# First attention: scores of two heads in the two halves of 64 rows of the matmul array

## The chip, the cores and the metric

The kernel runs on one core of one Trainium2 chip. The metric is the device time of one execution in microseconds (us). TensorE (PE) multiplies, VectorE (DVE), ScalarE (ACT) and GpSimd (POOL) work on what it leaves in PSUM and on SBUF, and SyncE (SP) and ScalarE issue DMA transfers.

## The reference, cut to what matters

Eight sequences of 512 tokens with 128 features pass through four layers, each an attention-like part and a feed-forward part. The first layer is

```
xn = layernorm(x)
q, k, v = xn @ wq.T + wq_b, xn @ wk.T + wk_b, xn @ wv.T + wv_b      # 16 heads of 8
q, k = rope(q), rope(k)
scores = einsum('bhqd,bhkd->bhqk', q, k) / sqrt(8)                 # no mask: 512 x 512 a head
attn = softmax(scores); out = einsum('bhqk,bhkd->bhqd', attn, v)
x = x + out * silu(ternary_ffn(xn))
```

Layers two and three have causal attentions of the same shape; layer three's feed-forward part is a local attention with 8 heads of 64; layer four has a router with 8 experts and a memory that is computed for all sequences at the end.

## The kernel before, in words

A loop runs over the 8 sequences. In each iteration `attention` (line 376) runs three times: first without a mask, then twice causal. Between them are `prepare` and the local attentions, and the iteration ends with `last_feed_forward` and `experts`. Each of these stages is a block of one instruction stream per engine. A block ends with a barrier of all engines, and `K.clear` (line 72) clears semaphores and holds a second barrier; so a stage lasts as long as its slowest engine, SP among them.

Scores are wanted in float32 accuracy at bf16 speed. q and k are split into three bf16 parts each, of 8 rows a head, and stored to DRAM (`parts_scratch`). `spread_loads` (line 326) then lays them into `K.qs` and `K.ks`: row 24i+8n+d of a head's slot holds part i of q and part n of k, so 72 rows give all 9 products of parts. Rows 72 and 73 hold ones in `ks` and, later, two bf16 parts of the row's negated maximum in `qs`. The 16 heads are 16 slots of 512 columns, in 4 groups of 4. A group takes 7 transfers: one of ones, three for q (each repeats one part of q three times), three for k. They are issued by SP in `experts` (line 2324) for the next sequence's first attention, by SP in `local_attention` (line 1364) and `attention` (line 572) for the causal ones, and before the loop, in `first_projections`, by ACT for k and ones (line 2082) and by SP for q (line 2091).

In the first attention TensorE goes through 50 steps. Each of the steps 0 to 31 has two *first scores* (line 446): 128 queries by 512 keys of one head over 72 rows, into banks 0 and 1 by turns, from which DVE takes the maximum (line 624); a first score waits until the maximum of the one two before it has been taken. Each of the steps 12 to 43 has two *second scores* (line 464): 128 keys by 512 queries over 74 rows, with the maximum already subtracted, into three banks, from which ACT takes the exponential (line 549). Within a step TensorE's order is first, second, first, second. Every odd step from 15 on ends with the product of the probabilities and v for four heads (line 510, `weigh`), in four strips of 32 columns of the array. At steps 9, 17, 25 and 33 the 16 maxima of a group are transposed (line 474); ACT and DVE split them in two parts (lines 540, 601), and SP puts them into row 72 and row 73 of `qs` by two transfers (line 577), for which the group's second scores wait. At steps 23, 31, 39 and 47 a group's output is transposed back (line 480). Beside this `TernaryFfn` (line 653) gives TensorE float32 products in steps 0 to 12 (line 678) and 36 to 39 (line 686). The order in which heads are taken is that of `items` for first scores (head by head, four tiles of queries each) and of the index for second scores (tile of keys by tile, four heads each).

In `experts` (line 2144) SP stores x, issues the 28 transfers of `spread_loads` and waits for the stores; TensorE ends with 8 filler matmuls (line 97), ACT with two stores, DVE with the last expert's sum.

## Time and profile before

| what | value |
|---|---|
| median of 3 runs | 4119.28 us (4107.81 to 4124.22) |
| the profiled execution: its own time, its span | 4109.15 us, 4107.4 us |
| mean granted TensorE clock | 0.96 |
| PE busy | 3458.5 us, 84% |
| DVE busy | 2573.8 us, 63% |
| ACT busy | 1774.8 us, 43% |
| POOL busy | 914.0 us, 22% |
| DMA | 140.06 MB, mean 34 GB/s |
| first scores, PE (line 446) | 1536 matmuls, 449.3 us, all three attentions |
| second scores, PE (line 464) | 1536 matmuls, 446.7 us, all three attentions |

Busy times are sums over the whole execution; engines work side by side, so they say which engine is full on average and not which one a stage waits for. A matmul's record covers its way through the array, so that the records of neighbours overlap: of a row of matmuls the distance of their starts is what each costs. "SPq" and "ACTq" rows are the issuing of a DMA by that engine's sequencer, not its transfer.

### The profile page before, as it was taken

How to read it: one execution, taken by the hardware profiler on the slowest of the kernel's cores; microseconds unless marked ns; L12 is line 12 of the kernel's file. 1: busy time of each engine (PE TensorE's matmuls, PEld its weight loads, DVE VectorE, ACT ScalarE, POOL GpSimd, SP SyncE). 2: the span in 40 equal slices, each digit the busy share in tenths (PEclk: the TensorE clock that was granted, in tenths of full speed). 3: DMA queues.
4: the chain of work that ended last, by engine and by line, in shares of the span. 5: the costliest groups of instructions: out<-in, count | busy, mean ns of one | idle time of the engine just before them, and what ended most of it. 6: DMA issues, size and time to landing. Idle time of an engine off the chain costs nothing. (4 is left out here: it accounts for less than half of the span.)

```text
span 4107.4 us, 55769 instructions
## 1 busy us (share of the span) xinstructions
PE 3458.5 (84%) x19522; PEld 1792.1 (44%) x19679; DVE 2573.8 (63%) x5560; ACT 1774.8 (43%) x3774; POOL 914.0 (22%) x793
## 2 busy tenths in 40 slices
PE   3988888888888889888888889888888889888867
PEld 1344444444344444444344443444434443444434
DVE  3567665666566755666656665566566666666655
ACT  1544434444444525444344434435254444444314
POOL 1023301332023400333013310224003230133114
PEclk9999999999999999999999999999999999999978
DMA  4000010001011020000111020110110000010230
GB/s 158 22 21 27 29 38 32 29 10 58 10 32 37 1 66 26 17 27 33 35 32 33 5 66 1 32 37 1 66 32 11 27 37 31 32 35 4 67 83 22
DMA packets 87847, 140.06 MB, mean 34 GB/s; under 512 B 12472, under 2 KB 62466, under 8 KB 85002
## 3 DMA queue, kind: packets, MB, share of 16 engines
q1 hardware_dynamic: 79250, 124.15, 9.4%
q10 hardware_dynamic: 8314, 12.21, 1.0%
q8 instruction: 169, 2.77, 0.3%
q14 instruction: 114, 0.93, 0.1%
HBM read 106.14 MB, written 29.39 MB: 33 GB/s over the span
## 5 line engine op out<-in xcount | busy, mean ns | idle before, releaser
L624 DVE TENSOR_REDUCE nmax<-banks 128x1 f32<-128x512 f32 (+3 forms) x1216 | 759.5, 658 | 420.9 <-PE banks L446 230.6
L549 ACT ACTIVATE probs<-banks 128x512 f32<-128x512 f32 (+3 forms) x1024 | 475.0, 526 | 292.8 <-PE banks L464 289.9
L446 PE MATMUL banks<-ks,qs 72*128 72x512 bf16 (+3 forms) x1536 | 449.3, 338 | 106.9 <-DVE nmax L624 70.9
L464 PE MATMUL banks<-qs,ks 74*128 74x512 bf16 (+3 forms) x1536 | 446.7, 336 | 46.4 <-ACT probs L549 16.6
L97 PE MATMUL banks<-filler,identb 128*128 128x512 bf16 x1584 | 413.1, 388 | 30.9 <-PEq L77 22.2
L446 PEld LDWEIGHTS banks<-ks,qs 72*128 72x128 bf16 x1536 | 142.1, 99 | 393.1 <-DVE nmax L624 225.6
L1498 ACT ACTIVATE probs<-banks,nm 128x192 f32<-128x192 f32 x512 | 172.9, 422 | 215.7 <-DVE nm L1450 215.7
L549 ACT ACTIVATE early<-banks 128x256 f32<-128x256 f32 (+3 forms) x512 | 193.3, 438 | 167.7 <-PE banks L464 165.1
L258 POOL TENSOR_TENSOR rstd<-var,neghalf 128x4 f32<-128x4 f32 (+1 forms) x16 | 21.3, 1329 | 1097.2 <-DVE var L209 1063.5
L97 PEld LDWEIGHTS banks<-filler,identb 128*128 128x128 bf16 x1728 | 168.0, 100 | 214.0 <-issue 73.3
L510 PE MATMUL banks<-probs,v 128*32 128x512 f32 (+3 forms) x2048 | 235.7, 532 | 27.4 <-POOL probs L590 18.2
L464 PEld LDWEIGHTS banks<-qs,ks 74*128 74x128 bf16 x1536 | 141.2, 100 | 242.4 <-ACT probs L549 76.4
L1532 POOL TENSOR_TENSOR probs<-probs,inv 128x768 f32<-128x768 f32 x128 | 187.3, 1467 | 256.4 <-DVE inv L1460 256.1
L590 POOL TENSOR_SCALAR_AFFINE_SELECT probs<-probs 128x512 f32<-128x512 f32 x128 | 97.7, 763 | 373.7 <-ACT probs L549 373.7
L452 PE MATMUL banks<-mask_q,identb 128*128 128x128 bf16 (+2 forms) x704 | 177.3, 252 | 0.0
L1457 DVE TENSOR_REDUCE total<-probs 128x4 f32<-128x768 f32 x128 | 121.9, 952 | 87.1 <-ACT probs L1498 84.2
L1399 PE MATMUL banks<-ident,probs 128*128 128x128 f32 x896 | 134.7, 283 | 36.9 <-ACT probsT L1509 20.0
L1450 DVE TENSOR_REDUCE nm<-banks 128x4 f32<-128x768 f32 x128 | 119.6, 934 | 61.9 <-PE banks L1380 61.9
L590 POOL TENSOR_SCALAR_AFFINE_SELECT early<-early 128x512 f32<-128x512 f32 x128 | 93.4, 729 | 288.4 <-ACT early L549 288.1
L1399 PEld LDWEIGHTS banks<-ident,probs 128*128 128x128 f32 x896 | 95.3, 141 | 79.1 <-POOL probs L1532 33.9
L678 PE MATMUL banks<-region,shared 128*128 128x512 f32 x256 | 127.9, 635 | 0.0
L678 PE MATMUL banks<-hid_b,shared 128*128 128x512 f32 x256 | 118.6, 595 | 2.8 <-ACT hid_b L697 2.8
(480 smaller groups left out, 6553.2 us busy)
## 6 DMA issues: line engine op xcount, KB each, us to landing
qs<-parts_scratch SPq DMA_DIRECT2D x300, 96.0 KB
ks<-parts_scratch SPq DMA_DIRECT2D x288, 96.0 KB
parts_scratch<-parts SPq DMA_DIRECT2D x50, 384.0 KB, 2.5
shared<-in_w_h SPq DMA_DIRECT2D x17, 1024.0 KB, 7.5
shared<-in_w SPq DMA_DIRECT2D x25, 256.0 KB, 3.0
qs<-max_parts SPq DMA_DIRECT2D x192, 4.0 KB
xn<-in_x SPq DMA_DIRECT2D x9, 256.0 KB, 2.7
factor_scratch<-g SPq DMA_DIRECT2D x9, 256.0 KB
```

What stands on the lines that cost most here:

```text
L97: nc.tensor.matmul(K.ps[:, bank, :], K.identb[:, :], K.filler[:, :], start=True, stop=True)
L446: mm = nc.tensor.matmul(K.ps[:, b, i * keys:(i + 1) * keys], K.qs[0:72, 4 * g + j, t * P:(t + 1) * P], K.ks[0:72, 4 * g + j, 0:keys], star ...
L452: mm = nc.tensor.matmul(diagonal, K.identb[:, :], K.mask_q[:, :].unsqueeze(1).to_broadcast([P, n_heads, P]), start=False, stop=True)
L464: nc.tensor.matmul(K.ps[:, b, q0:T], K.ks[0:KR, h, k * P:(k + 1) * P], K.qs[0:KR, h, q0:T], start=True, stop=True).then_inc(scored2, 1)
L510: mm = nc.tensor.matmul(K.ps[32 * j:32 * j + 32, 5, q0:T], K.v32[:, k, 4 * g + j, :], probs[:, 4 * (q % QUADS) + j, q0:T], start=(k == 0), ...
L549: nc.scalar.activation(probs[:, 4 * (q % QUADS) + m % 4, q0:T], K.ps[:, bank("second", m), q0:T], ACT.Exp, scale=scale).then_inc(exped, 1)
L590: nc.gpsimd.affine_select(diagonal, diagonal, [[0, 4], [1, P]], ALU.is_ge, 0.0, base=0, channel_multiplier=-1).then_inc(masked, 1)
L624: nc.vector.tensor_reduce(nmax[:, t, h:h + len(heads)], K.ps[:, n % 2, 0:len(heads) * keys].rearrange("p (j k) -> p j k", k=keys), AX.X, A ...
L678: mm = nc.tensor.matmul(K.ps[:, 6 + n % 2, :], w[:, k, c * P:(c + 1) * P], src[:, k, :], start=(k == 0), stop=(k == 3))
L1399: mm = nc.tensor.transpose(K.ps[:, 4 + e, o:o + P], probs[:, w % RING, e, i, (k - t + 1) * P:(k - t + 2) * P], K.ident[:, :])
L1498: a = nc.scalar.activation(probs[:, w % RING, e, i, 64:256], K.ps[:, 2 * u + e, 256 * i + 64:256 * i + 256], ACT.Exp, bias=nm[:, u, e, i:i ...
L1532: nc.gpsimd.tensor_tensor(x, x, inv[:, w % 2, :, :].rearrange("p e t -> p (e t)").unsqueeze(2).to_broadcast([P, 4, SPAN]), ALU.mult).then_ ...
```

## The change

The first attention's operands are laid out in two halves of 64 partitions. Heads 0 and 1 of a group are in rows 0 to 63, heads 2 and 3 in rows 64 to 127, two slots a group. A half holds 7 products of parts (q0 with k0, k1, k2; q1 with k0, k1, k2; q2 with k0) in 56 rows, and the ones and the maximum in 2 rows. First scores contract over 56 rows, second scores over 58, each with a `tile_position` that names its half. The order of heads changes so that neighbours on TensorE lie in different halves by turns: per step first (half 0), second (half 1), first (half 1), second (half 0). `spread_loads_by_half` replaces `spread_loads` in `experts` and `first_projections`: 14 transfers a group, each for two heads. The maxima go in by 4 transfers a group. The causal attentions keep `spread_loads`, 72 and 74 rows, and their order.

```diff
+HALF_ROWS = 7 * HD
+def half_rows(j, n, first=0):
+    return slice(64 * (j // 2) + first, 64 * (j // 2) + first + n)
+def half_slot(g, j):
+    return 2 * g + j % 2
+def spread_loads_by_half(nc, K, engine, queries=True, keys=True):
+    engine.wait_ge(K.saved, 32)
+    for g in range(NG):
+        slots = slice(2 * g, 2 * g + 2)
+        for e in range(2):
+            heads = slice(4 * g + 2 * e, 4 * g + 2 * e + 2)
+            part = lambda m: K.parts_d[m].rearrange("i (d h) t -> i d h t", d=HD)[:, :, heads, :]
+            if keys:
+                engine.dma_start(K.ks[half_rows(2 * e, 2, HALF_ROWS), slots, :],
+                                 K.ones_d[:, slots, :]).then_inc(K.spread[g], 16)
+            for i, n in enumerate((3, 3, 1)):
+                rows = half_rows(2 * e, HD * n, 24 * i)
+                if queries:
+                    engine.dma_start(K.qs[rows, slots, :], part(0)[i].unsqueeze(0).to_broadcast([n, HD, 2, T])
+                                     ).then_inc(K.spread[g], 16)
+                if keys:
+                    engine.dma_start(K.ks[rows, slots, :], part(1)[0:n]).then_inc(K.spread[g], 16)
...
-    QUADS, LAG, KR = 3, 12, 74
+    QUADS, LAG = 3, 12
+    KR, SPREAD, ROWS = (74, 7 * 16, 2 * 16) if causal else (HALF_ROWS + 2, 14 * 16, 4 * 16)
+    HEADS = (0, 1, 2, 3) if causal else (2, 0, 3, 1)
...
-        items = [(t, (j,)) for j in range(4) for t in range(NT)]
+        items = [(t, (j,)) for pair in ((0, 2), (1, 3)) for t in range(NT) for j in pair]
...
+                            half, slot = half_rows(j, HALF_ROWS), half_slot(g, j)
+                            mm = nc.tensor.matmul(K.ps[:, b, 0:T], K.qs[half, slot, t * P:(t + 1) * P],
+                                                  K.ks[half, slot, 0:T], start=True, stop=True,
+                                                  tile_position=(64 * (j // 2), 0))
...
-                    g, (k, j) = m // 16, divmod(m % 16, 4)
+                    g, k, j = m // 16, m % 16 // 4, HEADS[m % 4]
...
+                        half, slot = half_rows(j, KR), half_slot(g, j)
+                        mm = nc.tensor.matmul(K.ps[:, b, 0:T], K.ks[half, slot, k * P:(k + 1) * P],
+                                              K.qs[half, slot, 0:T], start=True, stop=True,
+                                              tile_position=(64 * (j // 2), 0))
...
+                            for e in range(2):
+                                sp.dma_start(K.qs[half_rows(2 * e, 1, HALF_ROWS + i), 2 * g:2 * g + 2, :],
+                                             mparts[2 * e:2 * e + 2, g % 2, i, :]).then_inc(rows, 16)
-                    sp.wait_ge(rows, 32 * (g + 1))
+                    sp.wait_ge(rows, ROWS * (g + 1))
...
-                spread_loads(nc, K, act, queries=False)
+                spread_loads_by_half(nc, K, act, queries=False)
...
-                spread_loads(nc, K, sp, keys=False)
+                spread_loads_by_half(nc, K, sp, keys=False)
...
-                spread_loads(nc, K, sp)
+                spread_loads_by_half(nc, K, sp)
```

The last three pairs are `first_projections` (ACT, SP) and `experts` (SP). The exponentials are written to the slot of `HEADS[m % 4]`, and `last_experts` waits for 14 transfers a group in place of 7.

## Rows read from the trace of the kernel before

**Rows 1.** Timeline of PE, 129.1 to 134 us: start us, length us, engine, line.

```profile
129.18 1.07 PE L510 MATMUL banks<-probs,v 128*32 128x512 f32 x8
130.18 0.39 PE L446 MATMUL banks<-ks,qs 72*128 72x512 bf16 x1
...
131.36 0.39 PE L446 MATMUL banks<-ks,qs 72*128 72x512 bf16 x1
...
131.96 0.39 PE L446 MATMUL banks<-ks,qs 72*128 72x512 bf16 x1
132.18 0.38 PE L464 MATMUL banks<-qs,ks 74*128 74x512 bf16 x1
132.49 1.06 PE L510 MATMUL banks<-probs,v 128*32 128x512 f32 x8
```

**Rows 2.** Timeline of DVE and of ACT in the same stretch.

```profile
130.61 2.48 DVE L624 TENSOR_REDUCE nmax<-banks 128x1 f32<-128x512 f32 x4 [0.82 <-PE banks L446]
...
130.89 2.37 ACT L549 ACTIVATE probs<-banks 128x512 f32<-128x512 f32 x4 [0.94 <-PE banks L464]
```

**Rows 3.** Timeline of PE in the first local attention, 338.1 to 339.3 us.

```profile
338.10 0.33 PE L1373 MATMUL banks<-mask_bands,identb 128*128 128x384 bf16 x1
338.35 0.92 PE L1380 MATMUL banks<-shared 64*128 64x192 f32 x8
339.21 0.33 PE L1399 MATMUL banks<-ident,probs 128*128 128x128 f32 x1
```

**Rows 4.** Timeline of PE in steps 0 to 11 of the first attention.

```profile
89.47 0.60 PE L446 MATMUL banks<-ks,qs 72*128 72x512 bf16 x2
89.91 1.88 PE L678 MATMUL banks<-region,shared 128*128 128x512 f32 x4
91.62 0.60 PE L446 MATMUL banks<-ks,qs 72*128 72x512 bf16 x2
```

**Rows 5.** DMA issues by line: duration ns min/median/max, first and last start us.

```profile
L337 SPq DMA_DIRECT2D qs<-parts_scratch x300: 675/697/828, 68.2 to 3879.3; - x150
L340 SPq DMA_DIRECT2D ks<-parts_scratch x288: 422/444/909, 192.5 to 3880.1; - x144
L333 SPq DMA_DIRECT2D ks<-ones_scratch x96: 243/256/356, 191.3 to 3876.6; - x96
L2693 ACTq DMA_DIRECT2D q_bd<-kvq_scratch x8: 436/442/444, 3937.8 to 3941.1; - x8
```

**Rows 6.** Timeline of the first `experts` stage and the start of the next attention.

```profile
531.62 0.35 SPq L333 DMA_DIRECT2D ks<-ones_scratch  x1
...
547.41 0.44 SPq L340 DMA_DIRECT2D ks<-parts_scratch  x1
...
555.78 2.35 PE L97 MATMUL banks<-filler,identb 128*128 128x512 bf16 x7 [0.22 <-issue]
...
560.01 0.60 PE L446 MATMUL banks<-ks,qs 72*128 72x512 bf16 x2 [1.88 <-PEq L77]
```

**Rows 7.** Timeline of ACT's issues in `first_projections` and the first attention's start.

```profile
71.25 0.26 ACTq L333 DMA_DIRECT2D ks<-ones_scratch  x1
...
77.61 1.22 ACTq L340 DMA_DIRECT2D ks<-parts_scratch  x3
80.47 1.28 ACT L697 ACT_TABLE_LOAD   x1 [8.54 <-PEq L77]
```

**Rows 8.** Timeline of the last group's maxima and second scores, 151 to 158 us.

```profile
153.32 1.19 SPq L577 DMA_DIRECT2D qs<-max_parts  x2
...
155.90 0.60 PE L464 MATMUL banks<-qs,ks 74*128 74x512 bf16 x2
```

**Rows 9.** SP's own waits, same stretch: us in total, times, longest.

```profile
SPq L429 <- DMA qs<-max_parts: 1.1, 1, 1.1
```

**Rows 10.** Stretches: us, busy PE, PEld, DVE, ACT, POOL, granted clock, DMA share, GB/s.

```profile
560.00:564.00 4.00, 3.99 (x7) 1.79 (x8) 1.29 (x2) 1.16 (x1) 0.00 (x0) 0.57 0.03 8
...
80.80:86.40 5.60, 5.54 (x8) 2.31 (x9) 1.29 (x2) 0.96 (x1) 0.00 (x0) 0.53 0.20 80
```

More of the change, by code:

```diff
@@ L441, in first_scores @@
                     if n % PER == 0:
-                        pe.wait_ge(K.spread[g], 7 * 16)
+                        pe.wait_ge(K.spread[g], SPREAD)
                     if n >= 2:
@@ L445, in first_scores @@
                     for i, j in enumerate(heads):
-                        mm = nc.tensor.matmul(K.ps[:, b, i * keys:(i + 1) * keys],
-                                              K.qs[0:72, 4 * g + j, t * P:(t + 1) * P], K.ks[0:72, 4 * g + j, 0:keys],
-                                              start=(i == 0), stop=not causal)
+                        if causal:
+                            mm = nc.tensor.matmul(K.ps[:, b, i * keys:(i + 1) * keys],
+                                                  K.qs[0:72, 4 * g + j, t * P:(t + 1) * P],
+                                                  K.ks[0:72, 4 * g + j, 0:keys], start=(i == 0), stop=False)
+                        else:
+                            half, slot = half_rows(j, HALF_ROWS), half_slot(g, j)
+                            mm = nc.tensor.matmul(K.ps[:, b, 0:T], K.qs[half, slot, t * P:(t + 1) * P],
+                                                  K.ks[half, slot, 0:T], start=True, stop=True,
+                                                  tile_position=(64 * (j // 2), 0))
                     if causal:
@@ L457, in second_scores @@
                 def second_scores(m):
-                    g, (k, j) = m // 16, divmod(m % 16, 4)
+                    g, k, j = m // 16, m % 16 // 4, HEADS[m % 4]
                     h, b = 4 * g + j, bank("second", m)
                     if m % 16 == 0:
-                        pe.wait_ge(rows, 32 * (g + 1))
+                        pe.wait_ge(rows, ROWS * (g + 1))
                     bank_read("second", m)
                     q0 = k * P if causal else 0
-                    nc.tensor.matmul(K.ps[:, b, q0:T], K.ks[0:KR, h, k * P:(k + 1) * P], K.qs[0:KR, h, q0:T],
-                                     start=True, stop=True).then_inc(scored2, 1)
+                    if causal:
+                        mm = nc.tensor.matmul(K.ps[:, b, q0:T], K.ks[0:KR, h, k * P:(k + 1) * P], K.qs[0:KR, h, q0:T],
+                                              start=True, stop=True)
+                    else:
+                        half, slot = half_rows(j, KR), half_slot(g, j)
+                        mm = nc.tensor.matmul(K.ps[:, b, 0:T], K.ks[half, slot, k * P:(k + 1) * P],
+                                              K.qs[half, slot, 0:T], start=True, stop=True,
+                                              tile_position=(64 * (j // 2), 0))
+                    mm.then_inc(scored2, 1)
                 beside.run(beside.on_tensor, -1)
@@ L538, in _ @@
                         if g >= 2:
-                            act.wait_ge(rows, 32 * (g - 1))
+                            act.wait_ge(rows, ROWS * (g - 1))
                         nc.scalar.activation(mparts[:, g % 2, 0, :], K.ps[0:4, bank("maxima", g), :],
@@ L548, in _ @@
                         q0 = k * P if causal else 0
-                        nc.scalar.activation(probs[:, 4 * (q % QUADS) + m % 4, q0:T], K.ps[:, bank("second", m), q0:T],
-                                             ACT.Exp, scale=scale).then_inc(exped, 1)
+                        nc.scalar.activation(probs[:, 4 * (q % QUADS) + HEADS[m % 4], q0:T],
+                                             K.ps[:, bank("second", m), q0:T], ACT.Exp, scale=scale).then_inc(exped, 1)
                     for q in weigh:
@@ L576, in _ @@
                     for i in range(2):
-                        sp.dma_start(K.qs[72 + i:73 + i, 4 * g:4 * g + 4, :], mparts[:, g % 2, i, :]).then_inc(rows, 16)
-                    sp.wait_ge(rows, 32 * (g + 1))
+                        if causal:
+                            sp.dma_start(K.qs[72 + i:73 + i, 4 * g:4 * g + 4, :],
+                                         mparts[:, g % 2, i, :]).then_inc(rows, 16)
+                        else:
+                            for e in range(2):
+                                sp.dma_start(K.qs[half_rows(2 * e, 1, HALF_ROWS + i), 2 * g:2 * g + 2, :],
+                                             mparts[2 * e:2 * e + 2, g % 2, i, :]).then_inc(rows, 16)
+                    sp.wait_ge(rows, ROWS * (g + 1))
                 if load:
@@ L1190, in _ @@
                 for g in range(NG):
-                    sp.wait_ge(K.spread[g], 7 * 16)
+                    sp.wait_ge(K.spread[g], 14 * 16)
         K.clear(spread=True, factor=False)
```

## The prediction

> **What bounds the kernel now.** I read the table of busy times first: PE is busy for 84%, which invites the thought that cheaper matmuls shorten the kernel. The timelines say where that holds. In steps 12 to 31 of the first attention, two steps and one `weigh` take 3.31 us (129.18 to 132.49) [rows 1]. TensorE comes out of the `weigh` at 130.18 and issues a first score, DVE begins its maximum at 130.61 [rows 2], and the third and fourth first scores start at 131.36 and 131.96, when DVE is done with the banks; DVE itself idles 0.82 us and ACT 0.94 us behind each `weigh` [rows 2]. So an interval is a loop over two engines: `weigh` (1.00), first score, maximum, first score (1.18), maximum (0.60), last pair and switch to the next `weigh` (0.53). In steps 0 to 11 TensorE alone sets the time, the scores standing between float32 products without a gap [rows 4]. From step 32 on ACT's exponentials and the last group's maxima do. The ends of the stages are the second place to read: `experts` ends when its last engine arrives at the barrier, and TensorE idles 1.88 us from its last filler to the next attention [rows 6].
>
> **TensorE's part.** Whether neighbours in the two halves run together is shown by the local attention, whose scores of 64 rows lie in halves: 8 records between 338.35 and 339.21, 0.86 us [rows 3]. A float32 record of 512 columns costs 0.43 (four in 1.71) [rows 4], so one of 192 costs 0.16; eight in a row would be 1.28. They do run in pairs. The same rows price the change of the array's shape: 384 columns of bf16 take 0.16, but 338.10 to 338.35 is 0.25, so about 0.09 is the switch; and from 132.18 to the `weigh` at 132.49 stand 0.31 for a matmul of 0.22, again 0.09 [rows 1].
>
> The Trainium skill (TensorEngine Tiling, Key Properties) says that a change of tiling mode drains the array. By that alone a pair placed between full-size products can be a loss; the 0.09 above is what this trace makes of it, and the sum below goes by the row.
>
> Steps 12 to 31 are 10 intervals. What stands between two waits for DVE gains nothing: the second score that runs beside the third first score only lengthens TensorE's wait. The last pair (131.96 and 132.18, then `weigh`) is on the loop, and its second matmul now costs nothing: -0.22 an interval. `weigh` has its own shape already, so no switch is added there. In the two intervals with a transposed output the chain runs through ACT, the transposes and DVE; I give them -0.1. Sum: 8 x 0.22 + 2 x 0.1 = -2.0 us. Between nothing and -2.2 is possible.
>
> Steps 0 to 11: a pair costs 0.44 now (89.47 to 89.91) [rows 4], after it 0.22 + 2 x 0.09 = 0.40. Twelve steps: -0.4 at most; a float32 product right behind a switch may lose some of that. I take -0.2.
>
> Steps 32 to 43: the last group's maxima are put into place by two transfers issued from 153.32 on, 0.60 each [rows 8], after which SP waited 1.1 us [rows 9]; they landed at 155.6, just ahead of the second scores at 155.90 [rows 8]. Four transfers land at 153.32 + 4 x 0.60 + 1.1 = 156.8. Then 0.9 us is on the path, and behind it come products of TernaryFfn that TensorE does without a gap, so nothing gives it back. Pairs between those products win 0.22 and pay two switches: nothing. +0.9. In the groups before, the same lateness falls into idle time of 0.82 and 0.94 us [rows 2]; nothing, or up to +0.5 each if that cover is gone.
>
> One first attention: -2.0 - 0.2 + 0.9 = -1.3 us, between -2.4 and 0. Eight: **-10 us** (-19 to 0).
>
> **SP's part, in `experts`.** This is the edit that looks free and isn't. A group is one issue of ones (0.26), three of q (0.70), three of k (0.44) [rows 5], with 0.05 between, 4.0 us; four groups ran from 531.62 to 547.85 [rows 6]. Now there are 56 issues. Is one of half the bytes cheaper? The row for `q_bd` says no: 32 rows of 2 KB cost 0.442, where 24 rows of 4 KB cost 0.444 [rows 5]. What does make it cheaper is few rows (ones, 2 rows: 0.256), and q pays more than k because of its repetition. So a half-group costs 0.30 + 2 x (0.75 + 0.49) = 2.8 for what is known, and the third product's q and k, 8 rows each and not repeated, cost between 0.30 each (as ones) and 0.75 + 0.49 (as now). I take the row of k for both, 0.98, as it is nearest in kind: 3.75 us, eight times 30.0. SP is done at 561.6; the ends are 558.8 and 563.7. Today's last arrival is the fillers' end, 555.78 + 2.35 = 558.13 [rows 6]. The stage ends 3.5 us later, between +0.7 and +5.6, and all engines wait for it. Nothing hides that: the cover of today was the 10 us between SP's last issue and the fillers. The transfers themselves are not late: the first group's are issued in the first 7.5 us, and group 1 is used 8 steps into the next stage. Eight stages: **+28 us** (+6 to +45).
>
> The longer gap costs clock as well. After 1.88 us without a matmul the next attention's first 4 us ran at a granted 0.57, a loss of 1.7 us; after the long gap before the loop it was 0.53 over 5.6 us, a loss of 2.6 [rows 10]. So up to 0.9 us in each of seven iterations; half of it, **+3 us**.
>
> **`first_projections`, once.** ACT issues 16 transfers from 71.25 to 78.83, and the next stage begins 1.64 us later, at 80.47 [rows 7]. With 32 it ends at 86.4 at the old price each; SP's 24 of q end before that. **+7 us** (+4 to +8).
>
> **Sum.** -10 + 28 + 3 + 7 = +28 us on the profiled execution's own 4109.15 us (span 4107.4, 1.75 around it): 4137. The median of the runs is 10 us above that execution, so I say 4119.28 + 28 = 4147 us, 0.7% slower.
>
> **Rivals.**
> *The issues stay hidden.* If SP's price fell with the bytes, the stage would end where it does now. The point from which this decides: 56 issues between 531.62 and 558.13, 0.47 each on average, where today's mix takes 0.58 with what lies between. For it: the 0.256 of ones. Against it: `q_bd` [rows 5]. It would leave -10 to -19 and up to +3 before the loop: 4105 to 4112, not slower. The Trainium skill (DMA: Bandwidth & Descriptors, Issuing engines are not separate DMA queues) speaks for it: the sequencer's time to start a DMA is usually small against the DMA. The rows of this case put it at 0.44 to 0.70 us, and here it is not the transfer that anybody waits for. 20%.
> *TensorE's gain counts in full.* 64 pairs of 0.22 are 14 us an attention, 113 in all; with +38 from above: 4044. It would need TensorE to set all the steps. The waits at 131.36 and 131.96 [rows 1] speak against it. 5%.
> *The change does not do what it says*: matmuls with bf16 operands in different halves do not overlap. Then the switches remain, 0.18 in 12 steps and at 8 groups of transposes, 3.6 us, with the late maxima 4.5 an attention: +36 + 38: 4193. Rows 3 are against it, though they are of float32 operands. 5%.
>
> **How the numbers follow.** 0.5% (20.6 us) is about what a measurement can tell from no change. The forecast has 70%; of its own spread (-19 + 6 + 4 to 0 + 45 + 6 + 8, that is 4110 to 4178) some 8 points lie within 0.5%, 62 above. The hidden issues give 18 points within and 2 below, the full gain 5 below, the failed overlap 5 above. Slower 0.67, same 0.26, faster 0.07. The range leaves out the two small rivals, half of the hidden issues' case and the dearest ends: 4110 to 4172.
>
> **What would show it.** In the changed profile: pairs of L446 and L464 starting within some 0.01 us of each other at the end of an interval, and intervals of 3.09 us. In `experts`, 24 rows of q and 24 of k a stage, their median for 2 KB rows still 0.70 and 0.44, the last near 561, and the next attention's first score some 31.9 us (now 28.4) behind the first issue of ones. Before the loop, the first score near 88 us. I am wrong if the issues of half size cost half, if those of 8 rows cost as little as ones, or if the intervals lose more than 0.22 because DVE finds its banks filled earlier.

## The result, and the profile after

| | before | after |
|---|---|---|
| median of the runs | 4120.50 us (4107.81 to 4124.22, 4 runs) | 4156.79 us (4148.34 to 4164.87, 4 runs) |
| ratio, 95% interval | | 1.0093 [1.0062, 1.0125] |
| profiled execution, its own time | 4109.15 us | 4152.53 us |
| its span | 4107.4 us | 4150.8 us |

The changed kernel is 0.9% slower; the forecast was 4147 us (4110 to 4172). The profiled span grew by 43.4 us. The first view to read is the sum over the whole span. The windows view of before, then of after (length; busy time and instructions of PE, PEld, DVE, ACT, POOL; granted clock; DMA share; GB/s):

```profile
0.00:4107.40 4107.40, 3458.52 (x19522) 1792.13 (x19679) 2573.76 (x5560) 1774.83 (x3774) 913.98 (x793) 0.96 0.11 34
```

```profile
0.00:4150.80 4150.80, 3448.20 (x19522) 1762.70 (x19679) 2574.51 (x5560) 1773.75 (x3774) 917.85 (x793) 0.95 0.10 33
```

The instructions are the same in number, PE's busy time fell by 10 us in all, and the granted clock fell with it. Summed over the clock's own records, TensorE stood at 1.2 GHz for 327 us before and for 402 us after.

**The loop of steps 12 to 31.** Timeline of PE in after, to be laid beside [rows 1]:

```profile
134.84 1.07 PE L556 MATMUL banks<-probs,v 128*32 128x512 f32 x8
135.84 0.39 PE L485 MATMUL banks<-ks,qs 56*128 56x512 bf16 x1
...
137.60 0.39 PE L485 MATMUL banks<-ks,qs 56*128 56x512 bf16 x1 [0.21 <-DVE nmax L676]
137.61 0.39 PE L508 MATMUL banks<-qs,ks 58*128 58x512 bf16 x1
137.93 1.06 PE L556 MATMUL banks<-probs,v 128*32 128x512 f32 x8
```

The last first score and its second score start 0.01 us apart (137.60, 137.61), where they stood 0.22 apart. The interval between two `weigh` is 3.09 us (134.84 to 137.93), where it was 3.31. DVE's idle time in it fell from 0.82 us [rows 2] to 0.60:

```profile
136.26 2.48 DVE L676 TENSOR_REDUCE nmax<-banks 128x1 f32<-128x512 f32 x4 [0.60 <-PE banks L485]
```

**Steps 0 to 11.** Timeline of PE in after, beside [rows 4]:

```profile
95.12 0.39 PE L485 MATMUL banks<-ks,qs 56*128 56x512 bf16 x2
95.44 1.98 PE L730 MATMUL banks<-region,shared 128*128 128x512 f32 x4
97.36 0.39 PE L485 MATMUL banks<-ks,qs 56*128 56x512 bf16 x2
```

The pair takes 0.32 us until the next product starts (it took 0.44), but the four float32 products now take 1.92 until the next pair (they took 1.71). A step of this form is 2.24 us and was 2.15.

**The last group's maxima.** Timelines of SP and of PE in after, beside [rows 8], and SP's own wait, beside [rows 9]:

```profile
158.09 2.38 SPq L628 DMA_DIRECT2D qs<-max_parts  x4
...
161.56 0.39 PE L508 MATMUL banks<-qs,ks 58*128 58x512 bf16 x2 [0.84 <-DMA qs<-max_parts]
```

```profile
SPq L462 <- DMA qs<-max_parts: 1.0, 1, 1.0
```

From the first issue to the second scores it is 3.47 us, where it was 2.58: 0.89 more, and TensorE stands idle for 0.84 of it.

**`experts`.** Timeline of the first `experts` stage in after, beside [rows 6]:

```profile
538.67 0.35 SPq L346 DMA_DIRECT2D ks<-ones_scratch  x1
...
541.64 0.29 SPq L351 DMA_DIRECT2D qs<-parts_scratch  x1
541.98 0.29 SPq L354 DMA_DIRECT2D ks<-parts_scratch  x1
...
563.28 1.67 PE L98 MATMUL banks<-filler,identb 128*128 128x512 bf16 x7
...
565.88 0.29 SPq L354 DMA_DIRECT2D ks<-parts_scratch  x1
...
568.40 0.39 PE L485 MATMUL banks<-ks,qs 56*128 56x512 bf16 x2 [3.45 <-PEq L78]
```

SP finishes at 566.17, 1.22 us behind the fillers' end (564.95), and TensorE idles 3.45 us to the next attention, where it idled 1.88. From the first issue of ones to the first score it is 29.73 us, and it was 28.39. The issues by line, beside [rows 5] (ns min/median/max):

```profile
L351 SPq DMA_DIRECT2D qs<-parts_scratch x216: 285/697/849, 66.7 to 3934.8; - x108
L354 SPq DMA_DIRECT2D ks<-parts_scratch x192: 295/434/484, 539.9 to 3935.1; - x192
```

The 24-row issues kept their price at half the bytes (median 697 ns; they were 697). Those of 8 rows, the third product's, cost 0.29 us each (541.64, 541.98).

This first stage of the kernel before, on which the prediction rests, is not like all its others. In four of its seven stages the last to arrive was not TensorE with its fillers but SP, which waits for the landing of ACT's 192 KB store of `aet`. The second stage of before, a timeline and SP's wait:

```profile
1030.75 1.67 PE L97 MATMUL banks<-filler,identb 128*128 128x512 bf16 x7
...
1037.36 1.28 ACT L697 ACT_TABLE_LOAD   x1 [10.35 <-PEq L77]
```

```profile
SPq L2169 <- DMA aet_scratch<-aet: 11.7, 1, 11.7
```

The fillers end at 1032.42, and SP waits 3 us longer. The store landed 2.4 to 4.4 us behind its issue in the seven stages of before, and 3.1 to 3.8 in those of after, where SP was in most stages still issuing.

**`first_projections`.** Timeline of ACT in after, beside [rows 7]. Its table load, which opens the first attention, moves from 80.47 to 86.25, and the first maximum from 81.5 to 86.9:

```profile
83.11 1.47 ACTq L354 DMA_DIRECT2D ks<-parts_scratch  x3
...
86.25 1.28 ACT L749 ACT_TABLE_LOAD   x1 [15.65 <-PEq L78]
```

**A stage whose code is the same in both.** The windows view of the second attention of the fifth iteration, before and then after:

```profile
2118.30:2197.30 79.00, 67.84 (x446) 34.91 (x452) 48.61 (x94) 38.09 (x92) 24.31 (x26) 0.94 0.02 8
```

```profile
2136.50:2222.80 86.30, 74.83 (x446) 37.69 (x452) 48.80 (x94) 38.53 (x92) 24.56 (x26) 0.84 0.02 8
```

The same 446 matmuls take 7.3 us longer, at a granted clock of 0.84 against 0.94; DVE's 94 instructions take what they took (48.6, 48.8). This stage's eight instances sum to 632.6 us before and 649.1 after.

With the span cut at the first maximum of each attention, at the layer norm and at x's store in `experts`, the 43.4 us fall so:

| part | before | after | difference |
|---|---|---|---|
| before the first maximum | 81.5 | 86.9 | +5.4 |
| 8 first attentions (time at 1.2 GHz) | 746.8 (21) | 755.7 (37) | +8.9 |
| 8 second attentions | 632.6 (82) | 649.1 (116) | +16.5 |
| 7 `experts` | 212.5 (55) | 219.1 (60) | +6.6 |
| all else | 2434.0 | 2440.0 | +6.0 |

The row of `experts` is the least firm. Single stages are longer, in both kernels: three of before's seven are above 30 us (one 34.3), and one of after's is 35.1. In a second execution of each kernel (below) the sums are 218.9 and 220.4.

### The profile page after: what moved, and what is told of

Read it like the earlier page. It is cut to its first block and busy times, and to the rows that moved or that the text cites. A ratio compares the mean times of both kernels' runs of the same rounds, so it can differ in the third digit from the quotient of the medians.

```text
span 4150.8 us, 56085 instructions
## 1 busy us (share of the span) xinstructions
PE 3448.2 (83%) x19522; PEld 1762.7 (42%) x19679; DVE 2574.5 (62%) x5560; ACT 1773.8 (43%) x3774; POOL 917.9 (22%) x793
## 5 line engine op out<-in xcount | busy, mean ns | idle before, releaser
L480 PE MATMUL banks<-ks,qs 72*128 72x128 bf16 (+3 forms) x1024 | 272.2, 319 | 72.8 <-DVE nmax L676 71.8
L504 PE MATMUL banks<-qs,ks 74*128 74x512 bf16 (+3 forms) x1024 | 268.1, 315 | 32.8 <-DVE max_parts L653 14.4
L259 POOL TENSOR_TENSOR rstd<-var,neghalf 128x4 f32<-128x4 f32 (+1 forms) x16 | 21.3, 1329 | 1121.0 <-DVE var L210 1086.1
L485 PE MATMUL banks<-ks,qs 56*128 56x512 bf16 x512 | 155.8, 392 | 63.7 <-PEq L78 36.0
L508 PE MATMUL banks<-qs,ks 58*128 58x512 bf16 x512 | 157.8, 388 | 27.0 <-ACT probs L595 19.5
L480 PEld LDWEIGHTS banks<-ks,qs 72*128 72x128 bf16 x1024 | 94.4, 101 | 192.6 <-DVE nmax L676 121.0
L504 PEld LDWEIGHTS banks<-qs,ks 74*128 74x128 bf16 x1024 | 94.6, 101 | 166.3 <-ACT early L595 41.6
L485 PEld LDWEIGHTS banks<-ks,qs 56*128 56x128 bf16 x512 | 36.7, 93 | 249.6 <-DVE nmax L676 137.2
```

The lines of the kernel that those rows point to most:

```text
L480: mm = nc.tensor.matmul(K.ps[:, b, i * keys:(i + 1) * keys], K.qs[0:72, 4 * g + j, t * P:(t + 1) * P], K.ks[0:72, 4 * g + j, 0:keys], star ...
L485: mm = nc.tensor.matmul(K.ps[:, b, 0:T], K.qs[half, slot, t * P:(t + 1) * P], K.ks[half, slot, 0:T], start=True, stop=True, tile_position= ...
L504: mm = nc.tensor.matmul(K.ps[:, b, q0:T], K.ks[0:KR, h, k * P:(k + 1) * P], K.qs[0:KR, h, q0:T], start=True, stop=True)
L508: mm = nc.tensor.matmul(K.ps[:, b, 0:T], K.ks[half, slot, k * P:(k + 1) * P], K.qs[half, slot, 0:T], start=True, stop=True, tile_position= ...
```

## The experiments

The theory after the first look: (A) the pairs overlap, DVE's loop gains 0.22 us; the late maxima, the steps 0 to 11 and SP's issues take more than that back; (B) a rival, that a large part of the 36 us is TensorE's clock falling more often in stages that the change does not touch. Each kernel is compared with runs of the kernel before on its own chip.

| kernel | median us | before us | ratio, 95% interval | first attentions | second attentions | `experts` | us at 1.2 GHz |
|---|---|---|---|---|---|---|---|
| `late_sp` | 4169.94 | 4113.89 | 1.0144 [1.0118, 1.0169] | 754.0 | 632.6 | 256.9 | 381 |
| `same_half` | 4196.17 | 4113.89 | 1.0229 [1.0185, 1.0274] | 800.1 | 647.0 | 215.2 | 409 |
| `two_max` | 4124.94 | 4113.89 | 1.0029 [1.0017, 1.0041] | 751.8 | 636.2 | 223.7 | 357 |
| `before_again` | 4112.47 | 4113.89 | 0.9998 [0.9986, 1.0010] | 747.1 | 637.7 | 218.9 | 354 |
| `after_again` | 4151.85 | 4105.45 | 1.0119 [1.0087, 1.0151] | 758.4 | 639.3 | 220.4 | 378 |
| `head_start` | 4145.74 | 4105.45 | 1.0104 [1.0072, 1.0135] | 755.1 | 641.8 | 215.1 | 388 |
| `more_fillers` | 4149.65 | 4105.45 | 1.0115 [1.0083, 1.0147] | 751.2 | 653.0 | 218.7 | 381 |
| `both` | 4110.51 | 4105.45 | 1.0009 [0.9993, 1.0026] | 746.9 | 635.1 | 219.5 | 337 |
| `four_max` | 4113.58 | 4111.58 | 1.0003 [0.9981, 1.0024] | 744.9 | 639.0 | 205.4 | 338 |
| `later_groups` | 4094.57 | 4111.58 | 0.9958 [0.9943, 0.9973] | 741.0 | 631.8 | 204.0 | 306 |
| `later_before` | 4113.47 | 4111.49 | 1.0005 [0.9989, 1.0021] | 738.7 | 650.7 | 203.2 | 374 |

Columns five to eight are of the one profiled execution of each.

### Do the pairs overlap: `same_half`

```diff
-        items = [(t, (j,)) for pair in ((0, 2), (1, 3)) for t in range(NT) for j in pair]
+        items = [(t, (j,)) for pair in ((0, 2), (1, 3)) for two in ((0, 1), (2, 3)) for j in pair for t in two]
-    HEADS = (0, 1, 2, 3) if causal else (2, 0, 3, 1)
+    HEADS = (0, 1, 2, 3) if causal else (0, 1, 2, 3)
```

> The changed kernel with another order of heads: the two first and the two second scores of a step all lie in the same half, so that no neighbours within a step can overlap; layout, transfers and switches stay. If the overlap is what shortens the interval of two steps from 3.31 to 3.09 us, it goes back to 3.31 here (7 intervals of 8 attentions, +12 us), and each of steps 0 to 11 costs 0.22 more (3.31 and 2.46 in place of 3.10 and 2.24; 12 steps of 8 attentions, +21 us): +33 us against the changed kernel, if the clock stays. If the interval was shortened by the smaller contraction or by the order of DVE's work instead, it stays 3.09 and the time within 10 us of the changed kernel's.

The end of an interval in `same_half`, the timeline of PE:

```profile
138.41 1.06 PE L556 MATMUL banks<-probs,v 128*32 128x512 f32 x8
...
141.18 0.39 PE L485 MATMUL banks<-ks,qs 56*128 56x512 bf16 x1
141.41 0.38 PE L508 MATMUL banks<-qs,ks 58*128 58x512 bf16 x1
141.71 1.06 PE L556 MATMUL banks<-probs,v 128*32 128x512 f32 x8
```

Neighbours in one half start 0.23 us apart and the interval is back at 3.30. The eight first attentions cost 44.4 us more than in after, where 33 were expected; instances with 3.4 us at 1.2 GHz took 99.0 us and 93.9, so 41 us are not the clock's. The overlap is real, and the smaller contraction did not shorten the interval. The third rival's figure (4193 us without overlap) is near the measured 4196 by luck: it had 4.5 us more an attention and 28 us for `experts`, and the runs have 6.7 us more an attention (800.1 against 746.8) and at most some 10 for `experts`.

### SP's lateness: `late_sp` and `head_start`

`late_sp` is the kernel before with SP made late:

```diff
                 spread_loads(nc, K, sp)
-                sp.wait_ge(stored, 48)
+                for i in range(38):
+                    sp.dma_start(K.ks[76 + 2 * (i % 24):78 + 2 * (i % 24), ...],
+                                 K.ones_d[...]).then_inc(stored, 16)
+                sp.wait_ge(stored, 48 + 38 * 16)
```

> The kernel before, with 38 more small transfers (ones into rows nobody reads) issued by SP behind the 28 of spread_loads in experts, so that SP comes to the stage's end as late as in the changed kernel (about 28 us behind the store of x, where it is 16.7 now); attention, first projections and layout are as before. Theory A (the 36 us come from the late SP, from 0.09 us a step in steps 0 to 11, from the late maxima and from the start, and the rest from TensorE's clock): experts gets some 1 us longer in seven iterations, 7 us, the first attention's stretch before the first weigh some 1 us longer by the clock, and the intervals stay 3.31; in all +7 to +20 us, the upper part only if the granted clock falls from 0.960. Theory B (the loss is in the attention alone): within 5 us of before, and the clock at 0.960.

Timeline at the end of the first `experts` stage in `late_sp`, and SP's wait there:

```profile
543.89 11.28 SPq L2326 DMA_DIRECT2D ks<-ones_scratch  x38
...
563.25 1.28 ACT L697 ACT_TABLE_LOAD   x1 [14.48 <-PEq L77]
...
566.18 1.03 PE L446 MATMUL banks<-ks,qs 72*128 72x512 bf16 x2 [10.33 <-issue]
```

```profile
SPq L2169 <- DMA ks<-ones_scratch: 6.0, 1, 6.0
```

The issues end at 555.17, just ahead of the fillers' end (555.85). What is late is the landing: SP waits 6.0 us for its own small transfers (4.8 to 7.2 in the seven stages), to 561.2, and ACT opens the next stage 2.1 us behind that. (TensorE's first score comes 2.9 us later still, an "issue" time that the profile doesn't explain and that other kernels show in single stages, too.) The seven stages grew by 44.4 us, 6.3 each: all engines wait for SP. But I had put SP's part down to issuing alone, and this run shows a second way to be late. I had expected +7 to +20 us of the 38 issues and got +56; the wait for the landing is what I missed. The first attentions, whose code is that of before, took 754.0 us in place of 746.8 and stood 35 us at 1.2 GHz in place of 21: a longer gap ahead of them costs clock in them.

`head_start` is after with the first half-group's seven issues moved ahead, to the end of SP's block in `last_feed_forward`:

```diff
                 nxt.store_parts(sp)
+                spread_loads_by_half(nc, K, sp, halves=range(1))
                 sp.wait_ge(gate_landed, 32)
...
-                spread_loads_by_half(nc, K, sp)
+                spread_loads_by_half(nc, K, sp, halves=range(1, 8))
                 sp.wait_ge(stored, 48)
```

> The changed kernel, with the first half-group's 7 transfers (3.4 us of SP's time) issued at the end of last_feed_forward's SP block, where SP waits for weights anyway. Theory A (SP ends 1.3 us behind TensorE's fillers in experts): from the store of x to the next attention's first maximum 29.3 us in place of 30.6, in 8 stages -10 us; what comes on top of that or against it is the clock's, up to 20 us. Rival (the stage is longer by the barrier and by code fetch and not by SP): the stage stays 30.6.

Timeline of `head_start` at the end of the first `experts` stage, then SP's wait, then the store's row among the DMA issues (its last number: median us from issue to landing):

```profile
562.21 0.45 ACTq L2286 DMA_DIRECT2D aet_scratch<-aet  x1
...
562.71 0.30 SPq L356 DMA_DIRECT2D ks<-parts_scratch  x1
...
563.52 1.68 PE L98 MATMUL banks<-filler,identb 128*128 128x512 bf16 x7
...
568.53 0.39 PE L487 MATMUL banks<-ks,qs 56*128 56x512 bf16 x2 [3.34 <-PEq L78]
```

```profile
SPq L2224 <- DMA aet_scratch<-aet: 3.4, 1, 3.4
```

```profile
aet_scratch<-aet ACTq DMA_DIRECT2D x1, 192.0 KB, 4.2
```

SP has issued all by 563.01, and the stage ends no earlier. Another wait stood behind the one removed: ACT's store of `aet` (192 KB), for which SP waits. It landed 4.2 us behind its issue here, and 2.4 to 4.1 us in the other six stages. So 7 stages gain only 4.0 us (219.1 to 215.1), about 0.6 each, where I had expected 1.3, and the whole is not told apart from after.

### The maxima: `two_max` and `four_max`

`two_max` is after with one transfer of four slots and stride 64 in the rows:

```diff
-                            for e in range(2):
-                                sp.dma_start(K.qs[half_rows(2 * e, 1, HALF_ROWS + i), 2 * g:2 * g + 2, :],
-                                             mparts[2 * e:2 * e + 2, g % 2, i, :]).then_inc(rows, 16)
+                            sp.dma_start(K.qs[HALF_ROWS + i:HALF_ROWS + i + 65:64, 2 * g:2 * g + 2, :],
+                                         mparts[:, g % 2, i, :]).then_inc(rows, 16)
```

> The changed kernel, with each part of a group's maxima put into both halves by one transfer (target rows 64 apart), 2 a group in place of 4. Theory A (late maxima are on the path in the last group): the distance from the weigh of step 35 to that of step 37 goes from 3.64 back to about 2.9 us, 0.8 us an attention, -6 us in all against the changed kernel. Rival (ACT's exponentials set that stretch anyway): the distance falls but the next ones grow, and the sum of all weigh distances stays 47.2 us.

Timelines of PE and SP in `two_max` at the last group's maxima:

```profile
159.31 1.06 SPq L627 DMA_DIRECT2D qs<-max_parts  x2
...
161.87 0.39 PE L508 MATMUL banks<-qs,ks 58*128 58x512 bf16 x2
```

2.56 us, as before, and no idle time in front of the second scores. That is 0.9 us in each of eight attentions, 7 us in all. The ratios say 26 to 37 us (1.0029 here, 1.0093 and 1.0119 for after, of 4115), and the mean clock is higher too, 0.957 to 0.959 against after's 0.948 to 0.955. One reading, that late maxima also pull the clock down, was put to the kernel before (in its first attention alone):

```diff
-                    for i in range(2):
-                        sp.dma_start(K.qs[72 + i:73 + i, 4 * g:4 * g + 4, :], mparts[:, g % 2, i, :]).then_inc(rows, 16)
+                    for i in range(2):
+                        for e in range(2):
+                            sp.dma_start(K.qs[72 + i:73 + i, 4 * g + 2 * e:4 * g + 2 * e + 2, :],
+                                         mparts[2 * e:2 * e + 2, g % 2, i, :]).then_inc(rows, 16)
```

> The kernel before with one edit: in the first attention each group's maxima are placed by four transfers of 2 slots in place of two of 4. Theory A (a late last group costs what it takes on the spot): the distance between steps 35 and 37 rises from 2.86 to about 3.6 us, 8 times, so 6 to 7 us in all; 4112 to 4119 beside a before of 4105 to 4113, ratio about 1.0016. Theory B (the late maxima also set back TensorE's clock in what follows, which the step from after to two_max, 32 us for some 7 us on the spot, allows): 15 to 30 us, ratio 1.004 to 1.007, and more than 82 to 92 us at the low clock in the untouched second attention.

Two first attentions in which the clock never fell, from `four_max` and from `later_before` (below), which has the code of before in this stage:

```profile
564.20:657.10 92.90, 86.84 (x397) 33.01 (x399) 48.76 (x92) 46.29 (x83) 0.00 (x0) 1.00 0.01 1
```

```profile
556.10:648.10 92.00, 86.76 (x397) 32.98 (x399) 48.76 (x92) 46.22 (x83) 0.00 (x0) 1.00 0.05 14
```

The late maxima cost 0.9 us an attention at full clock. The whole did not move by a measurable amount (1.0003): seven of this kernel's eight first attentions had no fall of the clock at all, where before had two in eight. The 7 us that the late maxima cost on the spot are thus hidden in the total by a clock that was rather better (0.957 to 0.964, where before had 0.951 to 0.962 on that chip). So the late maxima do not pull the clock down as a rule, and the rest of `two_max`'s gain is not shown to be theirs.

### How far one kernel differs from itself: `before_again` and `after_again`

Both are the kernels unchanged.

> The kernel before, unchanged, profiled once more beside the others. Nothing but the clock can differ: if TensorE's granted clock varies with the execution, time and clock move together (some 0.001 of the mean clock for each 3 to 4 us at most); theory A wants this kernel's clock near 0.960 and the changed one's near 0.950 in every execution, the rival (luck of one execution) wants both to scatter over the same values.

> The changed kernel, unchanged, once more. So far: the second attention, whose code is untouched, took 649.1 us over eight iterations in its trace against 632.6 before, with 116 us at the low clock against 82. Theory A (when in an iteration the clock falls depends on where a stage begins, and that is given by the iteration's length, so it recurs in each execution): 4145 to 4165 us, clock 0.948 to 0.953, the second attention again some 645 to 650. Rival (luck of that execution): the second attention near 635 and the median nearer 4140.

The ratio of after stands at 1.0119, as before. But the second attentions took 639.3 us in this execution of after (649.1 in the first), and 637.7 in this one of before (632.6). The same code's eight instances spread over 10 us from one execution to another. My expectation that after would show 645 to 650 again failed. Over the four runs of after, the time moves with the mean clock: 4148.34 us at 0.953, 4152.53 at 0.952, 4161.05 at 0.949, 4164.87 at 0.948.

The mean clock as such nearly tells the kernels apart: 0.948 to 0.955 in the eight executions of after, 0.953 to 0.960 in the ten of `before_again`. What recurs is a lower clock in the whole; in which stage it falls does not recur. The 69 executions of before that were timed beside the experiments give an estimate of its price: a straight line through them has 3.0 us for each 0.001 of mean clock. At equal mean clock by that line, after stands 22 us above before in both sets of four, `two_max` 12 above, `later_groups` 8 below and `later_before` 6 below. The single executions scatter by some 4 us around the line.

### Buying clock: `more_fillers`

```diff
-                keep_busy(nc, K, 0, 8)
+                keep_busy(nc, K, 0, 16)
```

> The changed kernel, with 16 fillers at the end of experts in place of 8, so that TensorE is busy until SP arrives. Theory A (the first attention's steps 0 to 11 lose about 1 us by 0.09 a step and another 0.5 us by the clock that fell in the longer gap): the clock's part goes, the first weigh comes some 0.5 us earlier behind the first maximum (40.7 in place of 41.2 on average), -4 us. Rival (it is the steps alone): no change in the first attention. If the fillers outlast SP, each stage gets up to 0.5 us longer.

The first attentions came down (755.7 to 751.2, 29 us at 1.2 GHz in place of 37), the second ones went up by as much (653.0, 119 us at 1.2 GHz). No gain.

### Both mended: `both`, `later_groups`, `later_before`

`both` is `two_max` and `head_start` together.

> The changed kernel with the maxima in 2 transfers and with the head start of SP. Theory A: 8 x (0.8 + 1.3) = 17 us off the changed kernel apart from the clock, that is what is left against the kernel before is 5 us at the start and 8 x 0.3 in the attention (0.09 a step in 12 steps against 7 intervals at -0.22 and some 0.2 behind the weighs): before +5 to +15 us. Rival (the clock outweighs it): not below the run with 2 transfers alone, 4125 us.

4110.51 us, level with before, and 41 us below after on the same chip, where 17 had been counted; the rest came with the clock (0.958 to 0.963 against 0.951 to 0.955). `later_groups` takes `two_max` and moves the issues of groups 2 and 3 out of `experts` and `first_projections`, into SP's idle time at the attention's start:

```diff
-def spread_loads_by_half(nc, K, engine, queries=True, keys=True):
+def spread_loads_by_half(nc, K, engine, queries=True, keys=True, groups=range(2)):
     engine.wait_ge(K.saved, 32)
-    for g in range(NG):
+    for g in groups:
...
                 if not fetched:
                     spread_loads(nc, K, sp)
+                if not causal:
+                    spread_loads_by_half(nc, K, sp, groups=range(2, NG))
```

> After with the two edits: maxima by two transfers of 4 slots per group, and the transfers of groups 2 and 3 issued by SP at the start of the first attention, where it was idle for some 30 us, so that experts and first_projections issue 28 each and not 56. If the prediction's terms for SP and the start are right and nothing else follows from them: first maximum at 81.5 as before (after 86.9), the seven experts stages at 212.5 or less (after 219.1), 12 to 17 us less than two_max: 4108 to 4113 beside a before of 4113.9, ratio 0.997 to 1.000. The rival: the loads in the first attention collide with the transfers of the feed-forward, and steps 0 to 11 grow by over 1 us each time: no gain, ratio 1.002 or more.

`experts` in `later_groups`, a timeline of SP and PE, and SP's wait:

```profile
539.83 0.29 SPq L354 DMA_DIRECT2D ks<-parts_scratch  x1
...
550.97 1.67 PE L98 MATMUL banks<-filler,identb 128*128 128x512 bf16 x7
554.52 0.39 PE L485 MATMUL banks<-ks,qs 56*128 56x512 bf16 x2 [1.88 <-PEq L78]
...
562.95 0.39 PE L485 MATMUL banks<-ks,qs 56*128 56x512 bf16 x2
```

```profile
SPq L2222 <- DMA aet_scratch<-aet: 11.9, 1, 11.9
```

SP is done 11 us before the fillers begin, the gap is 1.88 again, as in [rows 6], and seven stages take 204.0 us. The first maximum is at 80.5. 4094.57 us, ratio 0.9958 [0.9943, 0.9973]: it beats both kernels. The counterpart has the same move without the pairs:

```diff
                 if not fetched:
                     spread_loads(nc, K, sp)
+                if not causal:
+                    spread_loads(nc, K, sp, groups=range(2, NG))
```

> The kernel before with one edit: the transfers of groups 2 and 3 for the first attention are issued by SP at that attention's start and not in experts and first_projections; scores and maxima as before. It is the counterpart of later_groups without the pairs of heads. If the pairs in the two halves are worth the 0.7 us an attention that stages without a drop of the clock show (92.0 before, 91.3 in later_groups), this kernel is slower than later_groups (0.9958 of before) by 6 us or more and stands at 0.998 to 1.000 of before. The rival: the gain of later_groups comes from where the loads are issued alone; then this kernel reaches 0.996 as well.

Moving the loads alone brings nothing in the total (1.0005), but not because nothing moved. In the profiled executions the seven `experts` stages fell from 212.5 us to 203.2, each to 29.0 or 29.1, and the first attentions from 746.8 to 738.7; the second attentions, whose code is unchanged, rose from 632.6 to 650.7, with 137 us at 1.2 GHz in place of 82. With half the loads out of `experts`, `aet`'s store landed in 2.3 to 2.5 us in all fourteen stages of `later_before` and `later_groups`.

With the pairs it is 0.9958, some 19 us less than without (0.9958 / 1.0005 = 0.9953). A first attention of `later_groups` at full clock:

```profile
554.90:646.20 91.30, 81.09 (x398) 27.85 (x398) 48.58 (x92) 45.98 (x83) 0.00 (x0) 1.00 0.04 12
```

PE is busy for 81.1 us and not 86.8, yet the stage is 0.7 us shorter (91.3, it was 92.0): of 5.7 us saved on TensorE, seven eighths fall into its waits. 8 x 0.7 = 5.6 us, about 0.1%, is the direct gain, and all that is shown to be the pairs'. The other 13 us between the two medians come with the clock: 306 us at 1.2 GHz against 374 in the profiled executions, where 18.9 of the 21.3 us between them lie in the second attentions (631.8 against 650.7). The mean clock was 0.959 to 0.963 in all nine executions of `later_groups` and 0.953 to 0.958 in all twelve of `later_before`, so this is not one execution's luck; at equal clock the two are 2 us apart. Why the kernel with the pairs kept the better clock is not shown.

## Why the prediction was right, and where it was not

The total held: 4147 forecast, 4156.79 measured, slower by more than 0.5%, inside the range. Its sign has the reason that it named: SP's issues and the late maxima eat the pairs' gain, and with both taken out (`both`) the loss is gone. That the size came so near is partly luck. The terms that it named for stages the change touches, 25 us without the clock, came to some 18, less than the 20.6 us that it took as the least a measurement can tell; what carried the time to 4156.79 was the clock, for which it had 3 us.

- **Steps 12 to 31, -0.22 an interval**: right to the hundredth (3.31 to 3.09, pairs 0.01 apart). The six plain intervals between two `weigh` of an attention did so, and what lies in front of the first `weigh` won some 0.3. The intervals with a transposed output stayed at 3.54 us, where I had given -0.1. It makes -1.6 an attention, not -2.0.
- **Steps 0 to 11, -0.2**: the wrong sign. I had priced the pair rightly enough (0.32 against my 0.40 and the old 0.44) and warned that a float32 product behind a switch may lose some of that. It loses more: 1.92 for four products that took 1.71. Eleven of the twelve steps cost +0.08 or +0.09, +0.9 an attention. `later_groups` shows the same 2.24 us step at full clock, so it is not a low clock. The Trainium skill (TensorEngine Tiling, Key Properties) warns that a change of mode drains the array; the trace agrees in sign, and its price here is 0.31 us for the two changes (0.10 ahead of the product behind the pair, 0.21 in the products after it) against 0.22 of overlap. `same_half` bears that out: the same step without the overlap took 2.45 us, 0.30 above before's 2.15.
- **The last group's maxima, +0.9**: right. 0.89 by the trace of after, 0.9 by `four_max` at full clock, gone in `two_max`.
- So one first attention: -1.6 + 0.9 + 0.9 = +0.2 where I had -1.3. Instances of like clock agree: those with 3.4 us at 1.2 GHz took 93.7 us before and, two of three, 93.9 after. Eight are some +2 us, not -10. **This is the first failed step.**
- **`experts`, +28**: **the second failed step is the price of the 8-row issues**, for which I took the row of k, 0.98 for the two, as nearest in kind. They cost nearly as little as ones (0.25), 0.29 each. A half-group took 3.41 us against 3.75, all 56 issues 27.5 against 30.0, and the stage's end moved by 1.3 us rather than 3.5. Of +28 at most about 10 are left: stages of 29.0 to 29.5 us became 30.5 to 30.9. The sums over seven are 6.6 apart, and 1.5 apart in the second pair of executions (218.9, 220.4), since before too has stages that are longer. The lower bound, +6, had that case in it, and the prediction named it as a way to be wrong. That the stage's end follows SP held (`late_sp`). What I had not named is that SP waits for landings as well, `aet`'s above all: I took the fillers as today's last arrival from one stage, and in four of before's seven it is that wait.
- **`first_projections`, +7**: +5.4 measured, mis-sized by the same 8-row issues.
- **The clock, +3**: of the +8.9 in the first attentions some 7 are left for the clock; they stood 37 us at 1.2 GHz against 21. But the larger part lies where I had not looked: in the second attentions, whose code is unchanged, +16.5 us in the profiled pair of executions.

The terms that have a place of their own sum to +5.4 + 10 + 2 = some 18 us (14 by the sums over seven stages), of 43 in the profiled executions and 36 between the medians; the estimate at equal mean clock, 22, is near that. The rest, 18 to 25 us, lies for the most part where the clock fell. What the runs show of it: the mean clock is lower in both sets of executions of after, while the stage in which it falls varies between executions of one kernel (632.6 and 637.7 in before, 649.1 and 639.3 in after); it does not come from the late maxima as such (`four_max`), nor does a shorter gap before the attention cure it (`more_fillers`, `head_start`). It went away with both mended (`both`, 337 us at 1.2 GHz; `later_groups`, 306), though `later_before`, whose first attentions have hardly a fall of the clock (5 us), has 374. Why TensorE falls to 1.2 GHz in one second attention for 7 us and in another for 27 stays open.

The rivals: hidden issues (4105 to 4112) did not come, but their deciding point was near. SP's mean issue had to be 0.47 us in the stage; 56 issues took 27.5 us (538.67 to 566.17), 0.49. The rival leant on the Trainium skill (DMA: Bandwidth & Descriptors, Issuing engines are not separate DMA queues), by which a sequencer's time to start one DMA is usually small against the DMA. No row here has the landing of these loads, so that comparison itself is not tested; what decided was the sum of 56 issues, which set the stage's end. The full gain (4044) is excluded, and so is the failed overlap, by the starts 0.01 us apart and by `same_half`.

## What to carry to other kernels

Overlapping TensorE's work pays only at the place where TensorE comes last in the loop: here 0.7 us of 5.7. Before counting its gain, count what the new layout asks of the queues, here twice as many issues at 0.49 us each where it was 0.58, and put these where the issuing engine idles; that and the maxima in two transfers made a loss of 0.9% a gain of 0.4%, of which about half (8 us) is left at equal mean clock. Time moves of less than 1% in a kernel whose TensorE changes its clock must be read from stages at equal granted clock, before a mechanism is looked for in them.

## What the runs showed of the hardware

- The issue of a load from DRAM by SP cost by the rows of its SBUF side, not by bytes: 24 rows 0.70 us with repetition and 0.44 without, at 2 KB as at 4 KB a row; 8 rows, not repeated, 0.29; 2 rows 0.25. The maxima's transfers, from SBUF to SBUF, are not of that kind: one row of them cost some 0.57 to issue, with 4 slots as with 2. Two that place 4 slots each in rows 64 apart took 1.06 us; four of 2 slots took 2.38.
- A pair of 56 rows in the two halves starts 0.01 us apart, and two in the same half 0.23.
- A 192 KB store by ACT landed in 2.3 to 2.5 us in all fourteen stages with half the loads moved out (`later_before`, `later_groups`), in 2.4 to 4.4 in before's seven, although SP's last issue was about 7 us ahead of the store, and in 3.1 to 3.8 in after's. 38 tiny transfers, issued in 11.28 us, landed 6.0 us after the last of them was issued.
- The clock in a stage of the same 446 matmuls was 0.94 in the execution of before and 0.84 in that of after, worth 7.3 us. The Trainium skill (TensorE: Matmul & The Clock Gate, The HAM clock gate) says that the gate's timing does not begin anew with the kernel, and so differs from run to run; the 10 us between the second attentions of two executions of after agree with that. Why the mean clock of after was the lower one in both of its sets stays open.
